# Loads of x tiles 4 to 7 held back until the first weight tiles have landed

## The reference

```python
x = L0_attn_x
xn = _layernorm(x, axis=-1)
s = _L0_attn_ref(xn, L0_attn_Wz, L0_attn_bz, L0_attn_Wh, L0_attn_bh)
g = _silu(_L0_ffn_ref(xn, L0_ffn_w_gate, L0_ffn_w_up, L0_ffn_w_down))
x = x + s * g
# _L0_ffn_ref: h = silu(xn @ wg.T) * (xn @ wu.T); return h @ wd.T   (hidden size 3072, weights int32)
# then layer 1: layernorm, attention of width 1024, a gated feed-forward, x + s * g
```

## Time and profile before

| | us |
|---|---|
| time, median of the runs shown | 1167.37 |
| time, lowest of the runs shown | 1166.59 |
| time of the profiled execution | 1166.48 |
| its span on the slowest core (core 5), first to last instruction | 1165.3 |
| spans of all eight cores | 1163.4 to 1165.3 |
| PE busy in that span | 1147.6 |

### The profile page before, as it was taken

The page is one execution under the profiler, slowest core; times in us unless marked ns, Lnnn a source line. Parts: engine busy times, 40 slices in busy tenths (PEclk is TensorE's granted clock), DMA queues, the critical chain, the costliest instruction groups (busy, mean ns, idle before and its releaser), DMA issues.

```text
span 1165.3 us, 15111 instructions; the slowest of 8 cores (1163.4 to 1165.3 us)
## 1 busy us (share of the span) xinstructions
PE 1147.6 (98%) x5382; PEld 524.7 (45%) x5382; DVE 514.4 (44%) x606; ACT 291.1 (25%) x365; POOL 172.5 (15%) x321
## 2 busy tenths in 40 slices
PE   5999999999999999999999999999999999999998
PEld 3444444444444444444444444444444444444444
DVE  4233331555656764225566885011134343343343
ACT  4211111122123111112212723533112133322310
POOL 3222221111111111111011122221000000011121
PEclk8999999999999999999999999999999999999999
DMA  9996688544554675545552678984010112455676
GB/s 215 211 148 97 92 126 182 109 109 101 114 112 73 130 160 77 84 85 99 111 108 52 93 125 156 153 154 117 1 19 19 37 37 46 87 117 118 139 177 168
DMA packets 91401, 126.90 MB, mean 109 GB/s; under 512 B 48192, under 2 KB 48448, under 8 KB 91328
## 3 DMA queue, kind: packets, MB, share of 16 engines
q0 software_dynamic: 35200, 77.61, 40.6%
q1 hardware_dynamic: 56128, 48.33, 15.7%
HBM read 159.47 MB, written 20.97 MB: 155 GB/s over the span
## 4 chain that ended last, share of the span: by engine, by line
PE 98%; DMA 2%; DVE 0%; ACT 0%; issue 0%; SPq 0%; DVEq 0%; ACTq 0%; POOLq 0%
PE PS L156 97%; DMA S<-wg 1%; DMA S<-xtok 1%; PE PS L293 0%; ACT S L281 0%; DVE S L160 0%; ACT S L309 0%; DVE S L284 0%; SPq L127 0%; DVE S L889 0%; DVEq L63 0%; ACTq L63 0%; POOLq L63 0%
## 5 line engine op out<-in xcount | busy, mean ns | idle before, releaser
L156 PE MATMUL PS<-S 128*128 128x512 bf16 x5264 | 1135.9, 379 | 1.3 <-DMA S<-wg 1.3
L156 PEld LDWEIGHTS PS<-S 128*128 128x128 bf16 x5264 | 515.0, 98 | 620.2 <-issue 5.4
L160 DVE TENSOR_TENSOR S<-S,PS 128x512 bf16<-128x512 bf16 x96 | 66.0, 688 | 179.6 <-PE PS L156 170.2
L404 ACT ACTIVATE S<-PS 128x512 bf16<-128x512 f32 x96 | 57.3, 597 | 259.0 <-PE PS L156 192.9
L855 ACT ACTIVATE S<-PS,CB 128x2048 bf16<-128x2048 f32 x16 | 31.5, 1968 | 182.4 <-DVE CB L850 182.4
L848 DVE TENSOR_REDUCE CB<-PS 128x1 f32<-128x1024 f32 x32 | 39.2, 1225 | 72.3 <-PE PS L156 72.3
L127 POOL DMA_DIRECT2D S<-x1s x32 | 17.3, 539 | 337.2 <-DVE S L889 313.1
L127 POOL DMA_DIRECT2D S<-wg x48 | 28.7, 598 | 232.6 <-PE PS L156 230.0
L480 ACT ACTIVATE S<-PS 128x512 bf16<-128x512 f32 x32 | 19.1, 597 | 172.9 <-PE PS L156 172.9
L748 DVE SCALAR_TENSOR_TENSOR S<-S,PS 128x1024 f32<-128x1024 f32 x16 | 19.5, 1221 | 80.8 <-PE PS L156 79.7
L160 DVE TENSOR_TENSOR S<-PS,S 128x512 f32<-128x512 f32 (+1 forms) x33 | 22.3, 676 | 66.9 <-PE PS L156 66.6
(11 more groups left out here) (72 smaller groups left out, 429.9 us busy)
## 6 DMA issues: line engine op xcount, KB each, us to landing
S<-wg POOLq DMA_DIRECT2D x48, 256.0 KB, 5.1
S<-wu POOLq DMA_DIRECT2D x48, 256.0 KB, 5.8
S<-wd POOLq DMA_DIRECT2D x16, 768.0 KB, 8.0
S<-xtok SPq DMA_DIRECT2D x16, 512.0 KB, 9.9
S<-xt SPq DMA_DIRECT2D x16, 512.0 KB, 16.1
x1s<-S SPq DMA_DIRECT2D x16, 512.0 KB, 2.6
S<-x1s POOLq DMA_DIRECT2D x32, 256.0 KB, 5.9
out<-S SPq DMA_DIRECT2D x31, 256.0 KB, 4.8
```

Of the source, the lines that this page charges most:

```text
L156: ins = te.matmul(dst, l, r, start=(i == 0), stop=(i == n - 1))
L160: return DVE.did(ve.tensor_mul(o, a, b))
L404: at = ACT.did(se.activation(sil, ps(bg), AF.Silu, scale=1.0 / 127.0))
```

## The change

SP issues only x0, the identity and x1 to x3 at the start. x4 and x5 are issued after w1 has landed, x6 and x7 after w3 has landed, and CB and ones behind those. The pair w6, w7 moves on POOL from behind the bias of x5 to behind the bias of x4.

```diff
         xk_load(0)
         i_tok = dma(SYN, ident[:], identd, i_sem)
-        for i in range(1, 8):
+        for i in range(1, 4):
             xk_load(i)
-        c_tok = dma(SYN, CB[:, 0:32], cb, c_sem)
-        c_tok = dma(SYN, ones[:], onesd, c_sem)
...
         POOL.after(xk_tok[1])
         w_pair()
         w_pair()
+
+        for i, k in ((4, 1), (6, 3)):
+            SYN.after(w_tok[k])
+            xk_load(i)
+            xk_load(i + 1)
+        c_tok = dma(SYN, CB[:, 0:32], cb, c_sem)
+        c_tok = dma(SYN, ones[:], onesd, c_sem)
         ln0_norm(0, True)
...
         ln0_stats(4)
         ln0_rstd(4)
         ln0_bias(4)
+        w_pair()
         ln0_norm(4, True)
         ln0_stats(5)
         ln0_rstd(5)
         ln0_bias(5)
-        w_pair()
```

## The result

| | before | changed |
|---|---|---|
| median of the runs, us | 1166.98 | 1173.11 |
| lowest run, us | 1166.12 | 1172.61 |
| profiled execution, us | 1166.48 | 1172.61 |
| its span on the slowest core | 1165.3 (core 5) | 1171.4 (core 1) |
| spans of all cores | 1163.4 to 1165.3 | 1168.5 to 1171.4 |

The changed kernel is slower: ratio 1.0055, interval 1.0035 to 1.0075. That is within 2%, but it is 6 us where I had forecast 0.75 us to the other side, and outside the range of 1163.3 to 1169.4.

The account below looks back on a forecast made before the run. PE, 98% of the chain that ended last, was taken as the bound. T5 on core 5 at 28.8 instead of 29.55 moved the end equally: 1166.48 - 0.75 = 1165.7 us, range 1163.3 to 1169.4.

Parts of the forecast that it names:

- That a shift of the head goes into the span one to one: PE up to T7: no further wait behind T7, so T7 sooner or later moves the span by the same amount.
- G0 sooner: First products on PE: G0 starts at 19.3 instead of 20.5, 1.2 us sooner, with ACT's copy of x2 coming last.
- The unloaded duration for w0 and w1: Weight loads in the head: 4.9 and 5.2 us from issue, so w0 lands at 14.8 and w1 at 15.9.
- The pace of a weight tile: w2 and w3 behind w1: 1.5 us each at 164 to 176 GB/s, landing at 17.4 and 18.9.
- The landing of x4: x4 on SP's queue: issued at 15.9 when w1 lands, landing at 21.0, bounds 19.8 and 21.8.
- Equal shares by that rule: DMA round-robin over POOL's and SP's queues: x4 lands at 21.8 and nothing is gained, 1166.5 us.
- The x4 chain of 7.8 us: From x4's landing over POOL and ACT to T5: 7.8 us, so T5 starts no sooner than 28.8.
- rival (b): Ahead of T5: w1 lands at 18.6, x4 at 23.7, T5 at 31.5, end 2.0 us later, 1168.5; chance 0.27.
- Rival (c): POOL's queue slow by itself: w1 still at 23.0, x4 at 27, T5 5.2 us later, 1171.7; chance 0.06.
- T6 as T5 plus 3.26: PE behind T5: T6 follows by 3.26 us as before, so at 32.1, with x6's load hidden.
- The moved pair: w6 and w7 on POOL between x4's bias and x5's 1/std: 1.7 us in which x5's chain stands.
- That cores without a slow clock come level at the forecast: Other cores at T5: held by the same x4 chain to 28.8, losing up to about a microsecond, not beyond the maximum.

Follow-up runs that it names:

- e4: Changed kernel with w4 and w5 issued on POOL behind the bias of x4 instead of behind that of x2; 1171.91 us, ratio 1.0043.
- e7: Changed kernel with one x tile at a time: x4 released by w1, then x5, x6, x7 each by the landing of the one before; 1178.54 us.
- e2: Changed kernel with the pair w6, w7 put back behind the bias of x5, x loads still held; 1173.55 us, ratio 1.0085.
- e1: Kernel before with only the pair w6, w7 moved behind the bias of x4, all x loads at the start; 1166.63 us, ratio 1.0001.
- e3: Changed kernel with x4 and x5 issued at the start again, only x6, x7, CB and ones held until w3 landed; 1173.05 us, ratio 1.0054.
- e6: Changed kernel with x0 to x5 issued at the start, x6 and x7 held until w1 landed; 1169.56 us, ratio 1.0022.
- e8: Changed kernel with x0 to x5 issued at the start, x6 held until w0 landed, x7 until w1; 1167.82 us, ratio 1.0005.

## Why the prediction was wrong

**That a shift of the head goes into the span one to one** was right: T7 later by 6.11, the span longer by 6.1. On all eight cores of the changed kernel 1128.1 to 1128.6 us are left from the start of T7 on.

**G0 sooner** was right in size from slowest core to slowest core, -0.94 against -1.2, with ACT's copy as the last wait, but there is luck in it: these are two different cores. Core 5 by itself went from 20.50 to 20.17, and the mean of the eight from 19.9 to 19.5. No core waited for w1 before U0, as forecast.

**The unloaded duration for w0 and w1** was somewhat short: w0 took 5.2 us (4.9 taken), w1 6.6 (5.2 taken), perhaps because w2 and w3 are queued right behind them, which was not tried. SP's wait ended at 17.48, not near 16 (15.6 to 18.9 over the cores). That is 1.6 of the 5.7 us by which x4 was late on core 1. The pace of a weight tile, 1.5 us, was short too: alone the queue moved 124 GB/s, 2.1 us a tile, so w2 and w3 were still under way when x4 was released.

**The landing of x4** is the step that failed. I took 5.1 us from issue to landing and 5.9 as the upper bound; it was 9.2 us, and 7.9 on the mean of the eight cores. That is the other 4.1 us. I had concluded from the landed tiles that SP's queue gets four fifths of the bytes: 2.1 MB of x against 0.52 MB of w0 and w1. But tiles in flight count as well: the queue table of the same stretch has 0.93 MB of weights, and 45.7% against 55.1% by time. And the stretch is not uniform, as the short tables under e4 and e7 show: nearly x alone at first, nearly weights alone at the end. No average of it, by bytes or by time, is the share that a load released among queued weights will get. Half of the engines, my upper bound, was not enough either, since x4 got none of them for 4 us. What the runs showed in place of the 5.1 us is that the duration follows the weights that are queued when the load is issued: 7.9 us with w2 to w5 (changed kernel), 5.3 with w2 and w3 only (e4).

The Trainium skill, "DMA: Bandwidth & Descriptors", section "Queues, rings and completion order", says that a DMA engine goes round-robin over the queues that have work. I had quoted it and set my miscounted row above it. The trace agrees with it from 21.8 to 26.7, where both queues moved packets, 65% and 36% of the time, and not for the 4 us behind the issue of x4. Equal shares by that rule gave 21.8, and the landing was 26.7.

**The x4 chain of 7.8 us** over POOL was near: 26.7 + 7.8 = 34.5, T5 started at 35.06, the half microsecond more being U1 at the slow clock. With x4 at 26.7 instead of 21.0, the prediction's own chain would have given 1171.4 for the profiled execution: 1166.48 + (34.5 - 29.55) = 1171.4, against the measured 1172.61. So the wait of rival (b) is what happened, x4 late and T5 behind it, at about three times the price that I gave it (2.0 us, 6.1 measured). Its reason was only a small part: it had w1 at 18.6 and x4 5.1 us behind, where w1 was at 17.4 and x4 9.2 behind. Rival (c) came near in number, x4 at 27 and 1171.7, but by luck: its cause, w1 still at 23.0, did not occur.

**T6 as T5 plus 3.26** missed 0.6 us on core 1. The order of ACT and DVE behind the normalisation of x4 makes T6 follow x4's landing by 12 us on its own. On core 4, where x4 was in time, x6 landed at 29.2 instead of at most 27.4 and T6 came at 34.81; x5 had landed 3.7 us behind x4, beyond the 3.2 that I allowed.

**The moved pair** was costed as lengthening the chain of x5 by 1.7 us. But e2 shows no gain in the time when it is undone, and e1 no loss by it alone.

**That cores without a slow clock come level at the forecast** was wrong: all eight lost, with spans of 1168.5 to 1171.4, and most lost some of their full clock (means of 0.995 to 0.999, where six cores had 1.000 before).

## What to carry to other kernels

To hold a transfer back until another has landed does not only move it: it puts it behind everything that the other queues have queued in the meantime, and its duration there is set mostly by their backlog, not by its size. Before releasing a load by a landing, count the tiles in flight and not only the landed ones, and read the queue table (MB and share of the engines' time of each queue) in stretches short enough to see when each queue moves anything at all. As a first estimate take the bytes that the other queue has still to move at the pace it has alone, plus the load's own time. Look at what is issued within a microsecond on either side: in e3 that order made 4.3 or 8.8 us. If the consumer has a deadline, issue that much ahead, and check the deadline of every tile that is held, not only of the first. Here the best version kept six of eight loads at the start, released the seventh 9 us before its landing, and still gained nothing that can be shown.

## What was not expected of the hardware

- A cast load of a weight tile (512 KB read, 256 KB written) took about as much of the DMA engines' time as a plain 512 KB load: alone 0.62 MB in 5 us at a share of 103%, 2.1 us a tile, and 1.5 us a tile at the 176 GB/s of the earlier trace rows, where an x tile took 2.0 us of them. Counted per byte written it is up to twice as dear.
- A load issued while the other queue kept the engines busy moved no packet for 2.0 to 4.3 us (x4 of the changed kernel, eight cores), and then had the larger share, 65% against 36% on core 1. An average over both parts, 35 and 70% over 9.2 us, hides this.
- Keeping PE at full clock through a stall of 6 us ahead of T5 brought nothing, since the stall was that of a chain on other engines, which also set the next start. The same slow clock behind T6, where no such chain hid it, cost 1.3 to 2.4 us (T6 to T7 5.58 to 6.76 us instead of 4.33, in e3, e6 and e8).
